# One ring of three PSUM banks for exponents and projection jobs, jobs of 256 columns, and the eighth C group half a chunk later

## What is computed

```
xs, z = split(h @ in_w); xs = silu(xs)
proj  = xs @ xproj_w
dt    = softplus(proj[:, :512] + dt_bias);  B, C = the last 2 x 64 columns of proj
A     = -exp(A_log)
each step of time:  dA  = exp(dt_t[:, :, None] * A)
                    hst = hst * dA + (dt_t * x_t)[:, :, None] * B_t[:, None, :]
                    y_t = einsum('bds,bs->bd', hst, C_t)
out = (y + xs * D) * silu(z) @ out_w
```

## Time and profile before

| what | us |
|---|---|
| median of 3 runs (5531.95 to 5535.1) | 5534.01 |
| profiled execution, its own time | 5537.5 |
| span of its core | 5535.8 |
| granted clock of PE, mean | 0.985 |
| PE busy (share of the span) | 5360.0 (97%) |
| DVE busy | 4737.6 (86%) |
| POOL busy | 3918.4 (71%) |
| ACT busy | 3368.7 (61%) |

### The profile page before, as it was taken

How to read it: one execution, slowest core, us unless ns; L and a number is a source line. 1 busy time by engine, 2 the same in 40 slices (tenths; PEclk the granted TensorE clock), 3 DMA queues, 4 the chain that set the end, 5 groups by cost and what they waited for, 6 DMA issues and landing times. The chain is left out here.

```text
span 5535.8 us, 127746 instructions
## 1 busy us (share of the span) xinstructions
PE 5360.0 (97%) x43632; PEld 2426.9 (44%) x43632; DVE 4737.6 (86%) x2419; ACT 3368.7 (61%) x11178; POOL 3918.4 (71%) x6629
## 2 busy tenths in 40 slices
PE   5999999999999999999999999999999999997898
PEld 3444444444444444444444444444444444443444
DVE  2898998989898998989898999989898998997433
ACT  4666666666666666666666666666666666564111
POOL 4777777787877777787877778787877778674221
PEclk8999999999999999999999999999999999998999
DMA  3111112111111112111111112111111111112552
GB/s 100 55 46 53 52 36 64 36 60 35 56 47 53 51 34 63 38 53 44 55 46 53 51 35 64 37 54 44 55 46 49 52 35 47 31 28 81 157 156 64
DMA packets 433131, 306.57 MB, mean 55 GB/s; under 512 B 215920, under 2 KB 336240, under 8 KB 432496
## 3 DMA queue, kind: packets, MB, share of 16 engines
q1 hardware_dynamic: 428272, 294.39, 17.8%
q10 hardware_dynamic: 4224, 4.19, 0.2%
HBM read 187.27 MB, written 111.15 MB: 54 GB/s over the span
## 5 line engine op out<-in xcount | busy, mean ns | idle before, releaser
L829 DVE TENSOR_TENSOR_SCAN b_hs<-b_dA,b_u 128x1024 f32<-128x1024 f32 x2048 | 4552.4, 2271 | 425.4 <-ACT b_u L755 351.8
L979 PE MATMUL b_ex<-b_dd,b_aw 32*128 32x512 f32 x8192 | 3081.6, 643 | 23.0 <-POOL b_dd L492 15.0
L737 ACT ACTIVATE b_dA<-b_ex 128x496 f32<-128x496 f32 x4096 | 2286.3, 588 | 254.2 <-PE b_ex L979 234.5
L968 PE MATMUL b_u<-b_ud,b_bw 32*128 32x256 f32 x16384 | 2344.8, 403 | 36.3 <-DVE b_hs L829 33.8
L968 PEld LDWEIGHTS b_u<-b_ud,b_bw 32*128 32x128 f32 x16384 | 1385.9, 184 | 1135.6 <-issue 697.8
L492 POOL TENSOR_TENSOR b_dd<-b_dr,b_mask 128x512 f32<-128x512 f32 x1024 | 1073.2, 1048 | 646.2 <-DVE b_hs L829 629.9
L998 PE MATMUL b_y<-b_hs,b_cw 128*32 128x256 f32 x16384 | 1261.3, 390 | 2.7 <-DVE b_hs L829 2.7
L755 ACT ACTIVATE b_u<-b_hin 128x32 f32<-128x32 f32 x1792 | 361.2, 202 | 1438.8 <-PE b_u L968 1040.8
L979 PEld LDWEIGHTS b_ex<-b_dd,b_aw 32*128 32x128 f32 x8192 | 1057.2, 183 | 161.3 <-ACT b_dA L737 104.0
L501 POOL TENSOR_TENSOR b_ud<-b_ur,b_mask 128x512 f32<-128x512 f32 x1024 | 1082.4, 1057 | 0.1
L998 PEld LDWEIGHTS b_y<-b_hs,b_cw 128*32 128x32 f32 x16384 | 348.6, 108 | 1196.7 <-issue 1150.2
(11 more groups left out here) (128 smaller groups left out, 2492.6 us busy)
## 6 DMA issues: line engine op xcount, KB each, us to landing
b_u<-scratch_ut SPq DMA_DIRECT2D x256, 128.0 KB, 2.9
scratch_y<-b_ysb SPq DMA_DIRECT2D x128, 256.0 KB, 2.3
scratch_xs<-b_xs SPq DMA_DIRECT2D x64, 256.0 KB, 2.2
scratch_sz<-b_sd SPq DMA_DIRECT2D x64, 256.0 KB, 3.3
scratch_dt<-b_sd SPq DMA_DIRECT2D x64, 256.0 KB, 2.0
scratch_ut<-b_uT SPq DMA_DIRECT2D x64, 256.0 KB, 2.3
b_ur<-scratch_ut SPq DMA_DIRECT2D x1024, 16.0 KB
b_dr<-scratch_dt SPq DMA_DIRECT2D x1024, 16.0 KB, 1.7
```

The source lines that it names most:

```text
L737: nc.scalar.activation(dA[:, j % NDA, h, :, 1:TC], src[:, :, 1:TC], ACT.Exp).then_inc(exp_done, 1)
L829: nc.vector.tensor_tensor_scan(hs[:, v, :, :, kp].rearrange("p d t -> p (d t)"), dA[:, j % NDA, :, :, :].rearrange("p h d t -> p (h d t)") ...
L968: ins = nc.tensor.matmul(dst[:, :, tb, :], bw[row(r), c % 2, tb, :], ud[row(r), j // 2 % NPR, tb, :, :], start=(tb == 0), stop=(tb == NTB ...
L979: nc.tensor.matmul(e[bank_of(2 * j + h)][:, :], aw[row(r), p % DIRS, v, :, :].rearrange("p b s -> p (b s)"), dd[row(r), j // 2 % NPR, :, : ...
```

## The change

- Banks. `NDT` becomes 3 and `b_job` goes. The steady jobs (those from `first_job(1)` on) and the exponents share the three banks. `share_banks` works out in Python, step by step, which bank each exponent and each job gets (the one free earliest by an assumed time) and who held it before; PE waits for that holder alone.
- Jobs. xz, dt and B/C jobs are split into one for each sample, of 256 columns: 31 jobs in a unit. An xz job's two matmuls are issued in one step, every third step. The four matmuls of a dt or B/C job are issued in two steps, followed by one without. The order and distances of all the side work are written anew, on PE, ACT and POOL: ACT's starts with step 0 now, and a take runs in the (last) step of its job; clamp waits for both halves; POOL's and ACT's third step of `log_part` and first step of `softplus` are set anew too (by the generators: ACT's steps 55, 67, 79 and 91, POOL's 56, 68, 80 and 92).
- C groups. Groups 0 to 6 of a half chunk are added up at k % 8 = 1 to 7 of the next one, group 7 in the first step of the one after.
- ACT reads y out after carry and decays instead of before them.
- SP's stores are divided otherwise over the seven places between the chunks' loads.

```diff
-        NDA, NPR, NM, NDT = 4, 4, 4, 2
+        NDA, NPR, NM, NDT = 4, 4, 4, 3
-        jb = pb("b_job", [P, T])
-        first_banks = [jb, e[0], e[1], y]
+        first_banks = e + [y]
-        GROUP_AT = {1: (0,), 2: (1,), 3: (2,), 4: (3, 4), 5: (5,), 6: (6,), 7: (7,)}
-        DT_JOB = (8, 10, 13, 15)
-        UT_JOB = (11, 14, 16, 17)
-        BC_JOB, BT_JOB, UNIT_JOBS = 9, 12, 18
+        DT_JOB = (16, 20, 24, 27)
+        UT_JOB = (22, 26, 29, 30)
+        BC_JOB, BT_JOB, UNIT_JOBS = 18, 23, 31
+        DT_SLOT = (48, 60, 72, 84)
+        UT_SLOT = (66, 78, 90, 98)
+        BC_SLOT, BT_SLOT = 54, 69
+        TURN_SLOT = (108, 112)
...
+        def share_banks():
+            free_at, held_by = [-9.0] * NDT, [None] * NDT
+            bank, before = {}, {}
+            def give(what, until):
+                n = min(range(NDT), key=lambda b: free_at[b])
+                bank[what], before[what] = n, held_by[n]
+                free_at[n], held_by[n] = until, what
+            for slot in range(-2, PASSES * JP):
+                for h in range(2):
+                    if slot + 2 < PASSES * JP:
+                        give(("e", 2 * (slot + 2) + h), slot + 0.9 + 0.25 * h)
+                p, j = divmod(slot, JP)
+                if 0 <= p < PASSES - 1:
+                    n, slots = job_slots(p + 1).get(j, (None, 0))
+                    if slots:
+                        give(("job", n), slot + slots + 0.2)
+            return bank, before
...
                 def clamp(q, i):
...
-                    pool.wait_ge(freed, first_job(q) + i + 1)
+                    pool.wait_ge(freed, first_job(q) + CB * i + CB)
...
                 def unit(q):
                     for i in range(SILUS):
                         clamp(q, i)
-                        yield from wait_steps(3)
+                        yield from wait_steps(2)
                         if i:
                             times_sigmoid(q, i - 1)
-                        yield
-                    yield from wait_steps(4)
+                        yield from wait_steps(4)
+                    yield
                     times_sigmoid(q, SILUS - 1)
-                    yield from wait_steps(2)
+                    yield from wait_steps(3)
                     for j in range(JB):
                         yield from softplus(q, j)
-                        yield from wait_steps((8, 10, 8, 12)[j])
+                        if j < JB - 1:
+                            yield from wait_steps(8)
...
-                        if j % HALF == 0 and half >= 2:
-                            read_y(half - 2)
                         if j >= STEPS:
                             put_carry(p, j)
                         if j + 2 < JP:
                             decay(p, j + 2)
                         elif not last:
                             decay(p + 1, j + 2 - JP)
-                        if j >= 3:
-                            next(side, None)
+                        if j % HALF == 0 and half >= 2:
+                            read_y(half - 2)
+                        next(side, None)
...
+                def free_bank(what):
+                    kind, n = what
+                    if kind == "e":
+                        pe.wait_ge(exp_done, exped_to(0, n))
+                    else:
+                        pe.wait_ge(freed, n + 1)
...
+                def project_xz(q, i, b):
+                    n = first_job(q) + CB * i + b
                     bank_free(n)
                     for k in range(MB):
+                        last = nc.tensor.matmul(job_bank(n)[:, 0:SEQ], win[:, k, i * P:(i + 1) * P],
+                                                hT[:, q % DIRS, k, b * SEQ:(b + 1) * SEQ], start=(k == 0), stop=(k == MB - 1))
+                    last.then_inc(full, 1)
+                def project(q, n, cols, b):
                     bank_free(n)
+                    for k in range(JB):
+                        ins = nc.tensor.matmul(job_bank(n)[:, 0:SEQ], wxp[:, k, cols], xs[:, k, b * SEQ:(b + 1) * SEQ],
+                                               start=(k == 0), stop=(k == JB - 1))
+                        if k == 1:
+                            yield
+                    ins.then_inc(full, 1)
...
-                    pe.wait_ge(exp_done, exped_to(p, 2 * j + h - NDT))
+                    what = ("e", 2 * (p * JP + j) + h)
+                    if bank_before[what]:
+                        free_bank(bank_before[what])
...
-                    if half:
-                        for g in GROUP_AT.get(k % HALF, ()):
-                            add_up(half - 1, g)
+                    if k % HALF and half:
+                        add_up(half - 1, k % HALF - 1)
+                    elif half >= 2:
+                        add_up(half - 2, QG - 1)
```

More of the change, by code:

```diff
@@ L284, in unit @@
                         put_xs(j)
+                    yield
                     put_sz(0)
+                    put_sz(1)
+                    if q + 1 < PASSES:
+                        hold(sp, sp_passed, full, base + SILUS * CB)
+                        load_win(q + 1)
                     yield
[L287 to L292, removed]
+                    put_sz(2)
+                    put_sz(3)
+                    hold(sp, sp_passed, freed, base + BC_JOB + CB)
                     sp.dma_start(scr["c"][q], bc[DS:2 * DS, :]).then_inc(c_stored, 16)
@@ L692, in unit @@
-                    yield
-                    yield from log_part(q, 2)
-                    yield from wait_steps(3)
-                    take_ut(q, 1)
-                    yield from wait_steps(6)
-                    take_dt(q, 3)
-                    yield
-                    yield from log_part(q, 3)
-                    yield from wait_steps(3)
-                    take_ut(q, 2)
-                    yield from wait_steps(10)
+                        next(last, None)
+                        yield
@@ L884, in project_dt @@
+                def project_dt(q, j, b):
+                    if j == 0 and b == 0:
                         pe.wait_ge(wxp_loaded, (q + 1) * 16)
                         pe.wait_ge(silu_made, q * SILUS + JB)
-                    for k in range(JB):
-                        ins = nc.tensor.matmul(job_bank(n)[:, :], wxp[:, k, j * P:(j + 1) * P], xs[:, k, :],
-                                               start=(k == 0), stop=(k == JB - 1))
-                        if k == JB - 1:
-                            ins.then_inc(full, 1)
-                        yield
@@ L893, in project_bc @@
-                def project_bc(q):
-                    n = first_job(q) + BC_JOB
-                    bank_free(n)
-                    for k in range(JB):
-                        ins = nc.tensor.matmul(job_bank(n)[:, :], wxp[:, k, DI:PW], xs[:, k, :],
-                                               start=(k == 0), stop=(k == JB - 1))
-                        if k == JB - 1:
-                            ins.then_inc(full, 1)
-                        yield
+                    yield from project(q, first_job(q) + DT_JOB[j] + b, slice(j * P, (j + 1) * P), b)
@@ new lines, in unit @@
+                    for j in range(JB):
+                        for b in range(CB):
+                            yield from project_dt(q, j, b)
+                            yield from wait_steps(2)
+                        if j == 0:
+                            for b in range(CB):
+                                yield from project_bc(q, b)
+                                yield from wait_steps(2)
+                        elif j == 1:
+                            turn_inputs(q, 0)
+                            yield from wait_steps(3)
+                            turn_b(q)
+                            yield from wait_steps(3)
+                        elif j == 2:
+                            turn_inputs(q, 1)
+                            yield from wait_steps(6)
+                        else:
+                            turn_inputs(q, 2)
+                            yield from wait_steps(8)
```

180 lines of the change are left out of this document (99 added, 81 removed).

## The result

| what | us |
|---|---|
| before, median of 12 runs (5530.04 to 5535.1) | 5532.84 |
| after, median of 12 runs (5514.17 to 5526.27) | 5518.95 |
| ratio, 95% interval | 0.9977, 0.9969 to 0.9986 |
| span of the profiled execution, before and after | 5535.8, 5515.8 |

The change gains 14 us, 0.23%, where 156 us were forecast: faster, but outside the range. The gain can be told from no change, hardly more.

The account below looks back on a forecast made before the run. Scans waiting for ACT's carry, delayed by side work, stood 33.3 us a pass above a 278.8 us floor; stall falling to 23.0 gave -154.5, last pass -4.8, head +3: -156, median about 5378 us, range 5200 to 5460.

Parts of the forecast that it names:

- I cost the tie at zero afterwards: PE's exponents waiting for ACT to empty their bank: with a third bank, no cost left.
- a free step wins 0.53 back: PE against the 2.18 us scan step: a job step loses 0.53 us, a step without a job regains it.
- that the ring does not loosen PE at all: Shared banks leaving PE as tied as before; only the even job spread remains, between forecast and rival 2; no own chance.
- xz stage 3.0: Steps 0 to 47: PE's late job steps and POOL's clamp stall 3.0 us a pass, bounds 2 and 5.
- dt stage, PE alone, 4.7: Steps 48 to 89: PE's job steps, two in three, stall 4.7 us a pass, bounds 3 and 8.
- Softplus waits 13.6: POOL waiting for ACT's last logarithm step four times a pass instead of once: 13.6 us a pass, bounds 2.2 and 16.
- rival 1: POOL's softplus waits cost little, 0.54 us each, 11.4 us less a pass: 5207 us; chance 0.20.
- Half chunk starts, 0.5: New waits at k = 0 from the moved C group and later y read: 0.5 us a pass.
- Last pass -4.8: Last pass, without jobs: moving the eighth C group removes the 0.30 us gap 14 times, -4.8 us.
- ACT's order, zero: ACT's takes in their job's own step, 0.3 us each, within the 1.0 us a step left; no term in the sum.
- rival 2: More waits between ACT and PE: 26 takes add 0.2 us each, +5.2 us a pass, 5456 us; chance 0.09.
- Rivals 3 and 4: PE's extra weight loads exposed: at 0.11 us each 5532 us, chance 0.03; in full 5645 us, chance 0.06.

Follow-up runs that it names:

- c_narrow_decay: a_late_mod with ACT raising only a quarter of the columns of each step's first decay in passes 1 to 15: 5255.13 us, ratio 0.9497.
- a_late_mod: Changed kernel with POOL's softplus two steps later, ACT's modulation one operation a step, and its banks marked held for four steps: 5314.66 us, ratio 0.9607.
- a_old_groups: Changed kernel with the old C groups (two at k = 4, none at k = 0) and y read before the carry: 5523.22 us, ratio 0.998.
- c_narrow_take: a_late_mod with ACT taking only 128 of the 256 columns of each dt job in passes 1 to 15: 5317.74 us, ratio 0.9614.

## Why the prediction was wrong, point by point

- **The floor and the place of the loss: right.** 2.178 us a step, and the last pass 278.9 us (forecast 279.5). The loss is again in the passes with side work.
- **The failed step: "I cost the tie at zero afterwards".** An exponent now waits for one three before it, the first decay of the step before. That decay ends 2.14 us after the step's injections, and a free step lasts 1.65 us. So PE stands about 0.5 us in the step that follows a free one, and the step is 3.21 us long (2412.92 to 2416.13) instead of 2.71. The prediction took the cover as ACT's 1.19 us of work a step, an amount; it should have added up when the first decay ends: 1.34 us to the carry, then some 0.8 of the 1.19. Both the 1.34 and the 1.19 stood in the earlier trace rows. The rule of "a free step wins 0.53 back" falls with it: the 0.53 us that a free step wins are lost again in the step behind it, whose y comes 0.5 us late. In after there are about nine such steps a pass from 48 to 90, and more in the xz stage. Measured by c_narrow_decay: 4.0 us a pass for 0.31 us of the 0.5; in proportion the whole would be 4.0 x 0.5/0.31 = 6.4, an estimate. The sentence behind the rivals, "that the ring does not loosen PE at all", was nearer to this than the forecast was, and had no number and no chance of its own.
- **xz stage 3.0: mis-sized.** Steps 16 to 47 stall 5.8 us. First_inputs' gap was right (1.17 us printed at 2363.64, forecast 1.1), but the gaps near the job steps cost 0.2 to 0.5 instead of 0.13. The step that failed is part of it: the short decay takes 1.2 us away. The rest is not explained by a run.
- **dt stage, PE alone, 4.7: the size was right, for part of it.** (Its four terms add up to 4.8.) Half of the loads left out is worth 4.2 us a pass, and PE's three steps still last 0.5 us more than three scans. The tie comes on top.
- **Softplus waits 13.6: right in kind and nearly in size.** 64 waits, 183.3 us (forecast some 60 and 150), and taking them away gains 12.1 us a pass against 4 x 2.9 = 11.6 for the waits themselves. The gaps behind one stand four in a row, as forecast, and are 0.50 to 0.74 us (forecast 0.6 to 1.1). The 64 waits put rival 1 out.
- **Half chunk starts, 0.5: mis-sized.** DVE waits 53.0 us for y, 3.5 us a pass. With the later softplus 34.5 us are left; the short decay brings 37.7 (a_late_mod) down to 26.0, so a part of it is the tie.
- **Last pass -4.8: about the right number, wrong cause.** It is 5.4 us shorter (284.3 to 278.9), by the third bank (a_old_groups); the pair of C groups does no harm with it. The forecast's "the pair at k = 4 goes" gave the gain to the other edit, and then charged the move with little; in after, move and pair are about even.
- **ACT's order, zero: missed 1.3 us a pass** at the transposes of x, which the prediction did not price at all: the change's own table gave their bank away a step early (a_late_mod; 7 x 2.5 us and what followed). The takes of 256 columns cost 0.38 us for a copy and 0.47 for each of the two operations of a dt take, within the bounds of 0.3 to 0.6 but above the 0.3 taken. Making each dt operation 0.1 us shorter gained nothing (c_narrow_take), and that speaks against rival 2 too.
- **Before the first scan +3:** it was +4.1 (114.8 to 118.9).
- **Weight loads hidden: right.** 1.06 us for the pair. Rivals 3 and 4 are out by this row; the 5518.95 us lies near rival 3's 5532, but for other reasons. The rule of the Trainium skill, "TensorE: Matmul & The Clock Gate", section "The mechanism", that a load overlaps only when its row group differs, is not borne out by this 1.06 us.

The sum: tie 6.4, transposes of x 1.3, softplus 12.1 instead of 11.6: 8.2 of the 8.9 us a pass that were missing. The 6.4 rests on the extrapolation just given. What is shown without it is 4.0 + 1.3 + 0.5 = 5.8; the other 3.1 us stay open.

The forecast's own range was also too narrow for its terms. Their bounds add up to a stall of 8 to 35 us a pass; the prediction took 15 to 29, and the measured 310.7 - 278.8 = 31.9 lies within the first and not the second.

## What to carry to other kernels

When a ring of buffers is made deeper, don't compare amounts of work; write down when the holder is released, counted from the start of a step, and compare it with the shortest step, not with the mean one. An engine with uneven steps, loaded and free, keeps what a free step wins only if the release comes before the free step's end. And set the distance between a producer and its reader on another engine for the worst step: one step more at one place was worth 3% here. Without it the change gained 14 us, with it 187.

## What was not expected of the hardware

The granted clock of PE fell to half, the 1.2 GHz level, in the middle of the passes. Windows of after, before and in such a stretch:

```profile
2523.00:2528.77 5.77, 4.34 (x32) 1.98 (x32) 3.83 (x3) 2.38 (x9) 5.61 (x7) 1.00 0.00 0
2528.77:2535.59 6.82, 6.82 (x44) 2.90 (x43) 5.34 (x3) 2.64 (x10) 6.58 (x12) 0.50 0.24 87
```

It begins just behind a place where PE waited for ACT, beside the fourth softplus of the pass; PE's rows there:

```profile
2527.75 1.12 PE L1044 MATMUL b_ex<-b_dd,b_aw 32*128 32x512 f32 x2 [1.11 <-ACT b_dA L798]
2528.80 1.08 PE L1063 MATMUL b_y<-b_hs,b_cw 128*32 128x256 f32 x8
2529.81 0.80 PE L1031 MATMUL b_u<-b_ud,b_bw 32*128 32x256 f32 x2
```

At the low level a y takes 1.01 us (2528.80 to 2529.81, by the starts) instead of 0.57 (2412.35 to 2412.92). After has such stretches of 3.4 to 6.8 us at about step 93 of each of passes 0 to 14, at about step 69 of eight of them, and at step 29 of two; the kernel before has seven in all its passes. With softplus two steps later five are left, at steps 5, 29 and 113, and the mean clock is 0.985 instead of 0.974. So the waits of POOL and most of the low clock went with the same edit. PE was busy for 4.34 of the 5.77 us before the fall shown. The Trainium skill, "TensorE: Matmul & The Clock Gate", section "A second HAM failure mode: psum-queue depth-cycling", tells of another kernel in which short idle times between groups of matmuls let the clock fall and rise again; this trace agrees as far as it goes, with the 1.11 us shown. What the stretches cost by themselves was not measured apart from the waits; it is within the 12.1 us a pass.
